# The third sort of a graph network kernel runs on into the first attention

## The chip, the cores and the metric

The kernel runs on one core of one Trainium2 chip. The metric is the device time of one launch in microseconds (us), the median of three runs. Engines are named as in the profile: PE is TensorE, DVE is VectorE, ACT is ScalarE, POOL is GpSimd, SP is SyncE.

## The reference

A graph has N = 3125 nodes with 64 features and E = 100000 directed edges (`src`, `dst`). Four layers run one after another, each on the normalised features and each added to them; the first is the one that matters here:

```
# layer 0: attention over all edges, both directions (200000 rows), 4 heads of 16
ngl, ngr = node_attr @ Wl.T, node_attr @ Wr.T
score = (att * leaky_relu(ngl[src] + ngr[dst], 0.2)).sum(-1)
alpha = softmax of score over the edges of one source node
out   = segment_sum(ngr[dst] * alpha, src)      # then an MLP with gelu, added to x
# layers 1, 2: three sums over neighbours (nbr_x of h, twice, and of the features)
nbr_x = segment_sum(h[src], dst) * inv_deg ;  nbr_r = segment_sum(edge_attr, dst) * inv_deg
# layer 3: attention again, over one direction, 8 heads of 64; its MLP and norms
```

## The kernel before

**The first attention.** Both directions of the edges are sorted by node and laid out in rows of 4 edges. 54 blocks (`NB0`) are worked off in order; a block is 8 rows of 4 edges in each of 128 partitions. For a block POOL issues 32 indirect DMAs (`gather`, L738), which fetch 128 rows of the node table each into one of four buffers `G0[:, r]`; SP loads the block's indices `jst` and own rows (`load_block`, L563, L564), ahead by three blocks; DVE computes scores, running maxima and weighted sums (`block0`, `scores`); ACT does the exponentials; SP stores the block. POOL may start block g when DVE has finished block g-4 (semaphore `av`), and when the `jst` of block g has landed. SP loads `jst` of block g once DVE has formed the own rows of block g-3 (semaphore `aow`, L1387).

**The third sort.** Before that, DVE sorts three arrays of 128 x 1024 keys with a bitonic network: two of them for the attention's rows, the third for layers 1 and 2. A sort is a list of 175 stages: compares within a partition (`compare`, L1203, L1206, L1212, each a few min and max instructions between two buffers), sign flips (L1220), and turns (`turn_over`, L1231, L1233), in which PE transposes the array through PSUM (L1855) and DVE copies it back. All of it stands in DVE's stream before block 0. The buffers of all three sorts are `SBL`, in the space of `oh`, and PE transposes into `acc`.

**The count matrices.** When the third sort has ended, SP stores the sorted keys (L584); POOL, after the gathers of blocks 0 to 2 and before those of block 3, fetches nine windows of them (`gather_keys`, L728); PE transposes these, and DVE takes them apart into the table `SD` (L1344 to L1355). From `SD` the attention's blocks make, beside their own work, 272 units: a comparison on DVE (`matrix_ones`, L1414), 8 products on PE (L1902), a copy and a store to `mt_dram` on ACT. Blocks also sum the edge attributes: 122 groups of records (`rec_ones`, L1423; on PE L1910). A block of the first 48 takes 5 units and 2 records; the last six take 6, 5, 5, 6, 5, 5 units and 4, 5, 4, 5, 4, 4 records. Blocks 4 to 47 are loops of four blocks on every engine; the first four and the last six are written out.

**The order inside a block on DVE** is: own rows (8 x L1387), then, once the 32 gathers have landed, L1437 to L1444 and the small ones up to L1408, then units (L1414), records (L1423), and, with ACT's exponentials, L1453, L1460 and the scan L1467. Nearly every DVE instruction waits for the one before it.

Of the kernel before, what the change touches and what calls it, by code (L numbers as in the profile page):

```python
# [22 lines left out]
P = 128  # L23
NC = -(-N // P)
# [3 lines left out]
EP = P  # L28
EC = 784
EF = E // EP  # L30
EX = E - EF * EP
GT = 8
# [47 lines left out]
UAT = (0, 5, 10, 15, 20)  # L80
UL = (0, 6, 11, 16, 22, 27, 32)
ULR = (0, 4, 9, 13, 18, 22, 26)
LAST = NB0 - 6
assert LAST % 4 == 0 and NU == UAT[4] * (LAST // 4) + UL[-1] and UAT[4] % 4 == 0 and 2 * LAST + ULR[-1] == NG
# [4 lines left out]
def build(nc, t, out):  # L89
# [3 lines left out]
    with ctx:  # L93
# [124 lines left out]
        KI = ohf_[:, 0:MT].bitcast(I)  # L218
        KI2 = OHXf[:, 6400:6400 + MT // 2].bitcast(I)
# [11 lines left out]
        TK = OHXf[:, 2048:2048 + NKB * TE]  # L231
# [157 lines left out]
        def spans(eng, n, ahead, step):  # L389
# [6 lines left out]
            with eng.Fori(1, whole) as i:  # L396
                for t in range(4):
                    at(i, t)
            for t in range(4 * whole, n):
                at(t // 4, t % 4)  # L400
# [13 lines left out]
        class Unit:  # L414

            def __init__(self, i, at):
                self.u, self.q, self.slot, self.turn = i * UAT[4] + at, at % 2, at % 4, i * (UAT[4] // 4) + at // 4

        def units_of(a):
            if isinstance(a.g, int) and a.g >= LAST:  # L420
                return [Unit(LAST // 4, k) for k in range(UL[a.g - LAST], UL[a.g - LAST + 1])]
            return [Unit(a.i, k) for k in range(UAT[a.t], UAT[a.t + 1])]

        class Recs:

            def __init__(self, i, at):
                self.g, self.r, self.q, self.turn = i * 8 + at, at % 4, at % 2, i * 2 + at // 4

# [42 lines left out]
        def _(sp):  # L471
# [111 lines left out]
            sp.wait_ge(S["sorted"], 3)  # L583
            sp.dma_start(keyd.rearrange("(p x) -> p x", p=P), SBL[l_at]).then_inc(S["lnd"], 16)  # L584
# [16 lines left out]
            spans(sp, NB0, 3, serve0)  # L601
# [58 lines left out]
        def _(gp):  # L660
# [126 lines left out]
        def _(act):  # L787
# [64 lines left out]
            def weights0(a):  # L852
# [17 lines left out]
                store_unit(ready)  # L870
# [45 lines left out]
        def _(v):  # L916
# [305 lines left out]
            def turn_over(bufs, m=None):  # L1222
# [3 lines left out]
                for q in range(dst.shape[-1] // 512):  # L1226
                    banks[0] += 1
                    v.wait_ge(S["stp"], banks[0])
                    o, i = dst[:, q * 512:(q + 1) * 512], acc[:, q * 512:(q + 1) * 512]
# [9 lines left out]
            def ordered(bufs, lg):  # L1239

                at[0] = 0
                for k in range(1, lg + 8):
                    m = k - lg
                    if m == 0:
                        signed(bufs, m)
                    if m > 0:
                        turn_over(bufs)
                        for q in reversed(range(m)):
                            compare(bufs, 1 << q, 1 << m if m < 7 else None)
                        turn_over(bufs, m if m < 7 else None)  # L1250
                    for q in reversed(range(min(k, lg))):
                        compare(bufs, 1 << q, 1 << k if k < lg else None)
                    if 0 <= m < 7:
                        signed(bufs, m)

            for l in range(2):
# [10 lines left out]
                ordered(SBL, LL)  # L1267
# [60 lines left out]
            v.wait_ge(S["lnd"], 2 * 16)  # L1328
            link(V.memset(SBL[0], float(NC << 19)))
            keys = SBL[0][0:EP, 0:EC]  # L1330
# [3 lines left out]
            empty(SBL[0], float(NC << 19))  # L1334
            V.memset(vdum[:, 1:2], 0.0).then_inc(S["cb"], 1)
            v.wait_ge(S["cb"], 1)
            ordered(SBL, LL)
# [4 lines left out]
            for k in range(2):  # L1342
                o = TK[:, k * 1024:(k + 1) * 1024].rearrange("p (k x) -> p k x", x=TE)
                link(V.tensor_tensor(o, o, cell14[:, k * 4:k * 4 + 4].unsqueeze(2).to_broadcast([P, 4, TE]), ALU.subtract))  # L1344
            o = TK[0:LASTP, (NKB - 1) * TE:NKB * TE]
            V.tensor_scalar(o, o, cell14[0:LASTP, NKB - 1:NKB], None, ALU.subtract).then_inc(S["sub"], 1)
            v.wait_ge(S["sub"], 2)
            whole = KI[:, 0:2 * P * (NKB - 1)].rearrange("p (k s e) -> p k e s", s=P, e=2)
            link(V.tensor_copy(whole, acc[:, :].rearrange("p (k e s) -> p k e s", e=2, s=P)))
            link(V.tensor_copy(KI[:, 2 * P * (NKB - 1):MT].rearrange("p (s e) -> p e s", e=2), pt[:, 0:2 * LASTP].rearrange("p (e s) -> p e s", e=2)))  # L1350
            of_unit = SD.rearrange("p (u o t e) -> p u o t e", o=2, t=GT, e=2)
            for o, val, op in ((0, 127, ALU.bitwise_and), (1, 7, ALU.logical_shift_right)):
                for h in range(2):
                    link(V.tensor_scalar(KI2, KI[:, h * (MT // 2):(h + 1) * (MT // 2)], val, None, op))
                    link(V.tensor_copy(of_unit[:, h * (NU // 2):(h + 1) * (NU // 2), o],  # L1355
                                       KI2.rearrange("p (u t) -> p u t", t=GT).unsqueeze(3).to_broadcast([P, NU // 2, GT, 2])))
            link(V.tensor_copy(iota_ps, iota1))
            link(V.tensor_copy(attb_ps, attb[:]))

# [67 lines left out]
            def block0(a):  # L1427
# [324 lines left out]
        def _(pe):  # L1752
# [99 lines left out]
            def turn_blocks(src, count, first=0):  # L1852

                for b in range(count):
                    last = nc.tensor.transpose(acc[:, (first + b) * P:(first + b + 1) * P], src[:, b * P:(b + 1) * P], ident[:])  # L1855
                    if b % 4 == 3:
                        last.then_inc(S["stp"], 1)

            def sort_turns(bufs, lg):

                at = lg * (lg + 1) // 2
                for m in range(1, 8):
                    turns[0] += 1
                    pe.wait_ge(S["srt"], turns[0])
                    turn_blocks(bufs[at % 2], 1 << (lg - 7))
                    at += 1 + m
                    turns[0] += 1
                    pe.wait_ge(S["srt"], turns[0])
                    turn_blocks(bufs[at % 2], 1 << (lg - 7))
                    at += 1 + lg  # L1870
                turns[0] += 1
                pe.wait_ge(S["srt"], turns[0])
                return at % 2

            for l in range(2):
                k = sort_turns(SBL, LL)
                assert k == l_at
# [4 lines left out]
            k = sort_turns(SBL, LL)  # L1882
            assert k == l_at
            pe.wait_ge(S["sub"], 1)
            for b in range(2 * (NKB - 1)):
                nc.tensor.transpose(acc[:, b * P:(b + 1) * P], TK[:, b * P:(b + 1) * P], ident[:])
            for e in range(2):
                last = nc.tensor.transpose(pt[:, e * LASTP:(e + 1) * LASTP], TK[0:LASTP, (NKB - 1) * TE + e * P:(NKB - 1) * TE + (e + 1) * P],
                                           ident[0:LASTP, 0:LASTP])
            last.then_inc(S["sub"], 1)  # L1890

            pe.wait_ge(S["moh"], 1)
            for k in range(4):
                nc.tensor.matmul(acc[:, k * 512:(k + 1) * 512], zrow[0:1, 0:P], zrow[0:1, :], start=True, stop=True, skip_group_check=True)

            def beside0(a):

                for c in units_of(a):
# [143 lines left out]
```

## Time and profile before

| | |
|---|---|
| median of 3 runs | 6147.66 us (6140.43 to 6149.96) |
| the profiled execution | 6139.35 us, of which the span is 6137.6 |
| busy: DVE, POOL, PE, ACT | 4092.7, 3783.2, 2661.9, 1253.9 us |
| gathers of the first attention | 1323.4 to 3713.8 us in the span |
| indirect gathers of both attentions (L738) | 2592, 1036 ns each in the mean |

All times inside the kernel are microseconds from the start of the span of one profiled execution. "Idle before" an instruction is the time in which its engine did nothing, with what ended it behind the arrow. "issue" stands for time in which nothing was waited for: for POOL the 0.30 us between two indirect DMAs.

### The profile page before, as it was taken

How to read it: one execution, taken by the hardware profiler on the slowest of the kernel's cores; microseconds unless marked ns; L12 is line 12 of the kernel's file. 1: busy time of each engine (PE TensorE's matmuls, PEld its weight loads, DVE VectorE, ACT ScalarE, POOL GpSimd, SP SyncE). 2: the span in 40 equal slices, each digit the busy share in tenths (PEclk: the TensorE clock that was granted, in tenths of full speed). 3: DMA queues.
4: the chain of work that ended last, by engine and by line, in shares of the span. 5: the costliest groups of instructions: out<-in, count | busy, mean ns of one | idle time of the engine just before them, and what ended most of it. 6: DMA issues, size and time to landing. Idle time of an engine off the chain costs nothing.

```text
span 6137.6 us, 56339 instructions
## 1 busy us (share of the span) xinstructions
PE 2661.9 (43%) x13332; PEld 1809.3 (29%) x13333; DVE 4092.7 (67%) x6865; ACT 1253.9 (20%) x4370; POOL 3783.2 (62%) x3760
## 2 busy tenths in 40 slices
PE   1785101011332322222222342677674577777746
PEld 0661101011322222222222242546453232332315
DVE  9778888886986776767676774232322576676655
ACT  0000000000111111111111110000000677777741
POOL 2777777776777777777777774000002777777730
PEclk6555555555555555555555555767685788888876
DMA  6221121211222222222222231435261222332230
GB/s 229 53 54 51 48 56 48 73 29 50 77 79 61 72 61 71 63 70 64 69 64 68 66 85 39 144 104 179 69 205 22 58 83 77 87 86 77 84 98 7
DMA packets 388365, 472.44 MB, mean 77 GB/s; under 512 B 212478, under 2 KB 248384, under 8 KB 381041
## 3 DMA queue, kind: packets, MB, share of 16 engines
q1 hardware_dynamic: 132624, 279.73, 13.8%
q0 software_dynamic: 114832, 129.82, 9.7%
q10 hardware_dynamic: 140752, 61.28, 3.5%
q14 instruction: 116, 0.94, 0.0%
q8 instruction: 41, 0.67, 0.0%
HBM read 291.34 MB, written 179.19 MB: 77 GB/s over the span
## 4 chain that ended last, share of the span: by engine, by line
POOL 58%; issue 21%; PE 9%; DMA 6%; DVE 5%; ACT 0%; POOLq 0%; DVEq 0%; ACTq 0%; SPq 0%
POOL arena L738 44%; POOL rec_dram L695 11%; PE acc L1959 4%; DMA oh<-mt_dram 2%; PE acc L1780 2%; DMA V<-in_edge_attr_dram 2%; DMA rec_dram<-V,rowst 1%; PE acc L1782 1%; PE acc L1943 1%; POOL own_dram L715 1%; POOL pdum L688 1%; POOL arena L765 1%; DVE arena L1579 1%; PE pt L1770 0%; POOL own_dram L769 0%
## 5 line engine op out<-in xcount | busy, mean ns | idle before, releaser
L738 POOL DMA_INDIRECT arena<-tab_dram,jst x2592 | 2685.8, 1036 | 778.3 <-issue 777.8
L695 POOL DMA_INDIRECT rec_dram<-V,rowst x784 | 866.1, 1105 | 229.9 <-issue 217.8
L688 POOL TENSOR_TENSOR pdum<-pdum 128x1 f32<-128x1 f32 x197 | 58.5, 297 | 1138.3 <-DVE arena L1607 864.6
L1902 PE MATMUL pw<-OHX 128*128 128x128 bf16 x1632 | 210.3, 310 | 1120.8 <-DVE OHX L1414 1120.8
L1902 PEld LDWEIGHTS pw<-OHX 128*128 128x128 bf16 x1632 | 156.9, 140 | 1172.3 <-DVE OHX L1414 859.7
L1910 PE MATMUL acc<-arena,oh 128*128 128x64 f32 x1952 | 427.1, 420 | 20.9 <-DVE oh L1423 20.7
L1910 PEld LDWEIGHTS acc<-arena,oh 128*128 128x128 f32 x1952 | 417.2, 330 | 34.9 <-issue 34.9
L900 ACT ACTIVATE arena<-arena,ew 128x64 f32<-128x64 f32 x1728 | 417.8, 333 | 33.3 <-PE acc L1983 33.3
L1437 DVE TENSOR_TENSOR arena<-arena,pt 128x1024 f32<-128x1024 f32 x108 | 131.8, 1221 | 431.7 <-DMA arena<-tab_dram,jst 429.4
L900 ACT ACTIVATE OHX<-arena,ew 128x64 f32<-128x64 f32 x1728 | 417.7, 333 | 2.5
L1983 PE MATMUL acc<-OHX,ident 128*128 128x512 f32 x432 | 253.7, 753 | 371.0 <-ACT OHX L900 371.0
L1855 PE MATMUL acc<-ident,oh 128*128 128x128 f32 x336 | 82.7, 427 | 752.3 <-DVE vdum L1224 752.3
L1212 DVE TENSOR_TENSOR oh<-oh 128x256 f32<-128x256 f32 x792 | 341.6, 431 | 37.8
L1855 PEld LDWEIGHTS acc<-ident,oh 128*128 128x128 f32 x336 | 65.9, 223 | 770.2 <-DVE vdum L1224 770.2
L855 ACT ACTIVATE arena<-dc 128x476 f32<-128x476 f32 x54 | 57.5, 1065 | 1143.3 <-DVE dc L1405 1143.3
L1959 PE MATMUL acc<-V,oh 128*128 x1440 | 234.7, 321 | 106.4 <-DVE arena L1579 86.5
L1579 DVE TENSOR_TENSOR arena<-arena,acc 128x192 f32 x360 | 127.6, 355 | 214.2 <-PE acc L1959 207.7
L1414 DVE TENSOR_TENSOR OHX<-iotab,OHX 128x2048 bf16<-128x2048 bf16 x204 | 249.7, 1224 | 28.0 <-DVE OHX L1414 15.6
L1983 PEld LDWEIGHTS acc<-OHX,ident 128*128 128x128 f32 x432 | 103.8, 248 | 520.1 <-issue 520.1
L825 ACT COPY V<-arena 128x8 f32 (+1 forms) x98 | 20.1, 205 | 1157.6 <-DMA rec_dram<-V,rowst 1080.5
L1902 PE MATMUL pw<-oh 128*128 128x128 bf16 x544 | 70.2, 310 | 386.2 <-DVE oh L1414 386.2
L1049 DVE TENSOR_TENSOR OHX<-iotab,arena 128x364 bf16<-128x364 bf16 x336 | 180.3, 536 | 64.5 <-DVE OHX L1049 17.9
(523 smaller groups left out, 6463.2 us busy)
## 6 DMA issues: line engine op xcount, KB each, us to landing
oh<-mt_dram SPq DMA_DIRECT2D x90, 512.0 KB, 3.6
arena<-tab_dram,jst POOLq DMA_INDIRECT x2592, 2.5
arena<-rec_dram SPq DMA_DIRECT2D x122, 288.0 KB, 3.6
mt_dram<-oh ACTq DMA_DIRECT2D x272, 128.0 KB, 1.7
oh<-mt_dram SPq DMA_DIRECT2D x75, 416.0 KB, 3.9
oh<-mt_dram SPq DMA_DIRECT2D x75, 384.0 KB, 4.0
rows_dram<-V SPq DMA_DIRECT2D x27, 1056.0 KB, 4.0
rows_dram<-arena SPq DMA_DIRECT2D x27, 1056.0 KB, 4.3
```

What stands on the lines that cost most here:

```text
L695: gp.indirect_dma_start(rec[:, :], bass.IndirectOffsetOnAxis(ap=rowst[:, q, k:k + 1], axis=0), recst[:, q, k, :], None).then_inc(S[f"scat{ ...
L738: gp.indirect_dma_start(hd.G[:, a.r, j, :], None, table[:, :], row_of(jst[:, a.r, j:j + 1])).then_inc(S[f"{x}g{a.r}"], 16)
L900: last = A.activation(V3r[vslot[f]][:, (k * H3 + h) * D:(k * H3 + h + 1) * D], G3[:, a.r, t, 0:D], ACT.Copy, scale=ew[:, a.q, t * H3 + h:t ...
L1049: V.tensor_tensor(paired(o[:, a:a + n]), iota_pairs(n, wide, EP), values[:, k, :].unsqueeze(2).to_broadcast([EP, n, wide // 2, 2]), ALU.is ...
L1212: V.tensor_tensor(o[r], a[r], b[r], op).then_inc(S["v"], 1)
L1414: V.tensor_tensor(paired(mones[c.slot].rearrange("p o t n -> p (o t) n")), iota_pairs(2 * GT, P), SD[:, bass.ds(c.u * (4 * GT), 4 * GT)].r ...
L1579: V.tensor_tensor(o, o, group_sum(g), ALU.add).then_inc(S["cadd"], 1)
L1855: last = nc.tensor.transpose(acc[:, (first + b) * P:(first + b + 1) * P], src[:, b * P:(b + 1) * P], ident[:])
L1902: last = nc.tensor.matmul(unit_bank(c.slot)[:, k // 2 * P:(k // 2 + 1) * P], mones[c.slot][:, 0, k, :], mones[c.slot][:, 1, k, :], start=k ...
L1910: last = nc.tensor.matmul(o, roh[:, c.q, k, :], RG[:, c.r, k, 0:D], start=False, stop=True, skip_group_check=True)
L1959: last = nc.tensor.matmul(group_sum(g), mring[:, slot, g * 4 + k, :], hsp[:, bass.ds(rows[g * 4 + k] * (3 * D), 3 * D)], start=k == 0, sto ...
L1983: last = nc.tensor.matmul(row_bank(2 * f + k // RK), ident[:], V3r[vslot[f]][:, k * 512:(k + 1) * 512], start=k % RK == 0, stop=k % RK == ...
```

## The change

The stages of the sort become a list. The third sort uses two buffers of its own, `SB3`, in the space of `OHX`, and PE transposes it into `pw`. Its first 104 stages (`SORT_FRONT`) stay ahead of block 0; the other 71 are spread over blocks 0 to 7 (`SORTED_IN`), 8 or 9 in each, between scores and records. SP stores the keys between its steps for blocks 7 and 8; POOL gathers the windows after block 11 (`KEYS_AT` = 12); they are turned and taken apart in three parts on DVE and PE in block 13 (`units_ready`, `units_turned`). Blocks 0 to 13 make no units; the 272 units are made in blocks 14 to 53, 6 or 7 in each, 7 in the last four. Records stay where they were. DVE, PE and ACT have all 54 blocks written out, without loops; POOL and SP keep theirs, split in two.

```diff
-UAT = (0, 5, 10, 15, 20)
-UL = (0, 6, 11, 16, 22, 27, 32)
+SORTED_IN, SORT_FRONT = 8, 104
+UNITS_AT, KEYS_AT = SORTED_IN + 6, SORTED_IN + 4
...
-        KI = ohf_[:, 0:MT].bitcast(I)
-        KI2 = OHXf[:, 6400:6400 + MT // 2].bitcast(I)
+        SB3 = [OHXf[:, k * SWL:(k + 1) * SWL] for k in range(2)]
+        KI, KI2 = [OHXf[:, k * 1024:(k + 1) * 1024].bitcast(I) for k in range(2)]
...
-        TK = OHXf[:, 2048:2048 + NKB * TE]
+        TK = OHXf[:, 4096:4096 + NKB * TE]
...
+        def unit_at(g):
+
+            return max(g - UNITS_AT, 0) * NU // (NB0 - UNITS_AT)
...
+        def sort_part(g):
+
+            rest = len(edge_sort) - SORT_FRONT
+            at_ = [0 if h < 0 else SORT_FRONT + rest * min(h, SORTED_IN) // SORTED_IN for h in (g, g + 1)]
+            return edge_sort[at_[0]:at_[1]]
...
         def first_attention(eng, body):
 
-            quads(eng, NB0, body, 0, LAST // 4)
-            for t in range(LAST, NB0):
+            for t in range(NB0):
                 body(Group(t // 4, t % 4))
...
-            sp.wait_ge(S["sorted"], 3)
-            sp.dma_start(keyd.rearrange("(p x) -> p x", p=P), SBL[l_at]).then_inc(S["lnd"], 16)
...
-            spans(sp, NB0, 3, serve0)
+
+            def store_keys():
+
+                sp.wait_ge(S["sorted"], 3)
+                sp.dma_start(keyd.rearrange("(p x) -> p x", p=P), SB3[l_at]).then_inc(S["lnd"], 16)
+            spans(sp, NB0, 3, serve0, SORTED_IN, store_keys)
...
-                quads(gp, n, rows)
+                if hd is heads0:
+                    quads(gp, n, rows, 0, KEYS_AT // 4)
+                    held[0] += KEYS_AT
+                    gather_keys()
+                    held[0] -= KEYS_AT
+                    quads(gp, n, rows, KEYS_AT // 4)
+                else:
+                    quads(gp, n, rows)
...
             def taken0(a):
 
-                if isinstance(a.g, int) and a.g == 3:
-                    held[0] += 3
-                    gather_keys()
-                    held[0] -= 3
                 after(gp, S["av"], a.g - 3)
...
-            ordered(SBL, LL)
-            assert at[0] == l_at
-            V.memset(vdum[:, 0:1], 0.0).then_inc(S["srt"], 1)
-            V.memset(vdum[:, 1:2], 0.0).then_inc(S["sorted"], 1)
-            v.wait_ge(S["tkg"], NKB * 16)
+            at[0] = 0
+            ordered(SB3, edge_sort[0:SORT_FRONT])
...
+            def sort_more(a):
+
+                at[0] = edge_at[0]
+                ordered(SB3, sort_part(a.g))
+                edge_at[0] = at[0]
+                if a.g == SORTED_IN - 1:
+                    assert at[0] == l_at
+                    V.memset(vdum[:, 1:2], 0.0).then_inc(S["sorted"], 1)
+
+            def units_ready():
+
+                v.wait_ge(S["tkg"], NKB * 16)
...
+                for part in range(3):
+                    v.wait_ge(S["sub"], 2 * part + 2)
...
+                    V.tensor_copy(ordered_, turned_).then_inc(S["sub"], 1)
+                    v.wait_ge(S["sub"], 2 * part + 3)
+                    for o, val, op in ((0, 127, ALU.bitwise_and), (1, 7, ALU.logical_shift_right)):
+                        link(V.tensor_scalar(KI2[:, 0:wide], KI[:, 0:wide], val, None, op))
+                        link(V.tensor_copy(of_unit[:, part * P:part * P + wide // GT, o],
+                                           KI2[:, 0:wide].rearrange("p (u t) -> p u t", t=GT).unsqueeze(3).to_broadcast([P, wide // GT, GT, 2])))
...
                 scores(heads0, a, st, summed)
+                if a.g < SORTED_IN:
+                    sort_more(a)
+                if a.g == UNITS_AT - 1:
+                    units_ready()
                 for c in units_of(a):
                     matrix_ones(c)
...
+            side[0] = 0
+            sort_turns(pw, SB3, edge_sort[0:SORT_FRONT])
...
             def beside0(a):
 
+                if a.g < SORTED_IN:
+                    sort_turns(pw, SB3, sort_part(a.g))
+                if a.g == UNITS_AT - 1:
+                    units_turned()
```

## Rows read from the trace of the kernel before

**Rows 1.** The page's part 4, the chain that ended last, by engine.

```profile
POOL 58%; issue 21%; PE 9%; DMA 6%; DVE 5%; ACT 0%; POOLq 0%; DVEq 0%; ACTq 0%; SPq 0%
```

**Rows 2.** POOL's waits, 1324 to 3715: total us, times, longest us.

```profile
POOL pdum L688 <- DMA jst<-meta_dram: 28.9, 1, 28.9
```

**Rows 3.** Timeline of POOL, 1323 to 3715: start, us, engine, line, operation.

```profile
1323.39 0.48 POOL L688 TENSOR_TENSOR pdum<-pdum 128x1 f32<-128x1 f32 x1 [5.37 <-DMA jst<-meta_dram]
...
1456.87 0.74 POOL L688 TENSOR_TENSOR pdum<-pdum 128x1 f32<-128x1 f32 x3
...
1467.88 0.91 POOL L728 DMA_INDIRECT OHX<-keys_dram,arena  x1 [0.30 <-issue]
1497.68 0.19 POOL L688 TENSOR_TENSOR pdum<-pdum 128x1 f32<-128x1 f32 x1 [28.89 <-DMA jst<-meta_dram]
...
3712.89 0.94 POOL L738 DMA_INDIRECT arena<-tab_dram,jst  x1 [0.30 <-issue]
```

**Rows 4.** Timeline of SP's queue, 1290 to 1560.

```profile
1436.95 0.33 SPq L584 DMA_DIRECT2D keys_dram<-oh  x1
...
1494.07 0.33 SPq L563 DMA_DIRECT2D jst<-meta_dram  x1
```

**Rows 5.** Timeline of DVE, 1311 to 1560.

```profile
1315.63 0.69 DVE L1231 COPY oh<-acc 128x512 f32<-128x512 f32 x1 [1.21 <-PE acc L1855]
...
1317.21 7.53 DVE L1212 TENSOR_TENSOR oh<-oh 128x256 f32<-128x256 f32 x16
...
1342.30 0.75 DVE L1220 TENSOR_SCALAR oh<-oh,sgn 128x1024 f32<-128x1024 f32 x1
...
1436.84 0.06 DVE L1340 MEMSET vdum<- 1x1 f32 x1
1470.42 2.49 DVE L1344 TENSOR_TENSOR OHX<-OHX,arena 128x1024 f32<-128x1024 f32 x2 [33.51 <-DMA OHX<-keys_dram,arena]
...
1491.46 2.59 DVE L1387 SCALAR_TENSOR_TENSOR pt<-pt,jst,arena 128x64 f32<-128x64 f32 x8
...
1528.03 2.59 DVE L1387 SCALAR_TENSOR_TENSOR pt<-pt,jst,arena 128x64 f32<-128x64 f32 x8
...
1558.80 1.29 DVE L1467 TENSOR_TENSOR_SCAN V<-arena 128x544 f32<-128x544 f32 x1
```

**Rows 6.** DVE's waits, 1324 to 3757.

```profile
DVE arena L1437 <- DMA arena<-tab_dram,jst: 429.4, 43, 11.0
```

**Rows 7.** The page's part 5: busy us, mean ns | idle before.

```profile
L1414 DVE TENSOR_TENSOR OHX<-iotab,OHX 128x2048 bf16<-128x2048 bf16 x204 | 249.7, 1224 | 28.0 <-DVE OHX L1414 15.6
```

**Rows 8.** Groups of POOL's instructions, 1396 to 1406, DVE comparing.

```profile
L738 POOL DMA_INDIRECT arena<-tab_dram,jst x8 | 9.2, 1155 | 2.4 <-issue 2.4
```

**Rows 9.** Groups of POOL's instructions, 1437 to 1457, DVE idle.

```profile
L738 POOL DMA_INDIRECT arena<-tab_dram,jst x16 | 15.1, 944 | 4.9 <-issue 4.9
```

**Rows 10.** Timeline of POOL, one gather beside DVE's L1220.

```profile
1342.65 1.22 POOL L738 DMA_INDIRECT arena<-tab_dram,jst  x1 [0.30 <-issue]
```

**Rows 11.** Groups of DVE's instructions, 1454 to 1498.

```profile
L1355 DVE CAST OHX<-OHX 128x2176 bf16<-128x2176 int32 x4 | 5.2, 1294 | 0.1
L1354 DVE TENSOR_SCALAR OHX<-oh 128x1088 int32<-128x1088 int32 x4 | 2.9, 727 | 0.1
```

**Rows 12.** Timeline of DVE, the last blocks (51, 52, 53).

```profile
3628.36 2.59 DVE L1387 SCALAR_TENSOR_TENSOR pt<-pt,jst,arena 128x64 f32<-128x64 f32 x8
...
3672.48 2.59 DVE L1387 SCALAR_TENSOR_TENSOR pt<-pt,jst,arena 128x64 f32<-128x64 f32 x8
...
3702.22 1.22 DVE L1423 TENSOR_TENSOR oh<-pt,arena 128x1024 f32<-128x1024 f32 x1 [2.19 <-PE acc L1910]
...
3711.86 2.59 DVE L1387 SCALAR_TENSOR_TENSOR pt<-pt,jst,arena 128x64 f32<-128x64 f32 x8
3716.24 2.47 DVE L1437 TENSOR_TENSOR arena<-arena,pt 128x1024 f32<-128x1024 f32 x2 [1.79 <-DMA arena<-tab_dram,jst]
...
3751.61 1.29 DVE L1467 TENSOR_TENSOR_SCAN V<-arena 128x544 f32<-128x544 f32 x1
```

More of the change, by code:

```diff
@@ L387, in quads, with spans @@
                     body(Group(n // 4, t))
-        def spans(eng, n, ahead, step):
+        def spans(eng, n, ahead, step, cut=4, between=None):
             def at(i, t):
@@ L395, in spans @@
                 at(0, t)
-            with eng.Fori(1, whole) as i:
-                for t in range(4):
-                    at(i, t)
+            for i, e in ((1, cut // 4), (cut // 4, whole)):
+                if i == cut // 4 and between:
+                    between()
+                if i + 1 == e:
+                    for t in range(4):
+                        at(i, t)
+                elif i < e:
+                    with eng.Fori(i, e) as turn:
+                        for t in range(4):
+                            at(turn, t)
             for t in range(4 * whole, n):
@@ L414, in build, with __init__ @@
         class Unit:
[L416 to L417 removed]
+            def __init__(self, at):
+                self.u, self.q, self.slot, self.turn = at, at % 2, at % 4, at // 4
         def units_of(a):
[L420 to L422 removed]
+            return [Unit(k) for k in range(unit_at(a.g), unit_at(a.g + 1))]
         class Recs:
@@ L427, in __init__, with sort_stages @@
                 self.g, self.r, self.q, self.turn = i * 8 + at, at % 4, at % 2, i * 2 + at // 4
+        def unit_at(g):
+            return max(g - UNITS_AT, 0) * NU // (NB0 - UNITS_AT)
+        def sort_stages(lg):
+            for k in range(1, lg + 8):
+                m = k - lg
+                if m == 0:
+                    yield "sign", 0, None
+                if m > 0:
+                    yield "turn", None, None
+                    for q in reversed(range(m)):
+                        yield "compare", 1 << q, 1 << m if m < 7 else None
+                    yield "turn", m if m < 7 else None, None
+                for q in reversed(range(min(k, lg))):
+                    yield "compare", 1 << q, 1 << k if k < lg else None
+                if 0 < m < 7:
+                    yield "sign", m, None
+                if m == 0:
+                    yield "sign", 0, None
+        edge_sort = list(sort_stages(LL))
+        def sort_part(g):
+            rest = len(edge_sort) - SORT_FRONT
+            at_ = [0 if h < 0 else SORT_FRONT + rest * min(h, SORTED_IN) // SORTED_IN for h in (g, g + 1)]
+            return edge_sort[at_[0]:at_[1]]
         def recs_of(a):
@@ L1237, in turn_over, with ordered @@
                 at[0] = 1 - at[0]
[L1239 to L1254, printed above, removed]
+            def ordered(bufs, stages):
+                for what, b, c in stages:
+                    if what == "turn":
+                        turn_over(bufs, b)
+                    elif what == "sign":
+                        signed(bufs, b)
+                    else:
+                        compare(bufs, b, c)
             for l in range(2):
@@ L1342, in _ @@
[L1342 to L1356, printed above, removed]
+            at[0] = 0
@@ L1850, in _, with turn_blocks, sort_turns @@
             turns = [0]
-            def turn_blocks(src, count, first=0):
+            def turn_blocks(into, src, count):
                 for b in range(count):
-                    last = nc.tensor.transpose(acc[:, (first + b) * P:(first + b + 1) * P], src[:, b * P:(b + 1) * P], ident[:])
+                    last = nc.tensor.transpose(into[:, b * P:(b + 1) * P], src[:, b * P:(b + 1) * P], ident[:])
                     if b % 4 == 3:
                         last.then_inc(S["stp"], 1)
[L1859 to L1870, printed above, removed]
+            side = [0]
+            def sort_turns(into, bufs, stages):
+                for what, _, _ in stages:
+                    if what == "turn":
+                        turns[0] += 1
+                        pe.wait_ge(S["srt"], turns[0])
+                        turn_blocks(into, bufs[side[0]], SWL // P)
+                    if what != "sign":
+                        side[0] = 1 - side[0]
+            for l in range(2):
+                side[0] = 0
+                sort_turns(acc, SBL, sort_stages(LL))
+                assert side[0] == l_at
                 turns[0] += 1
                 pe.wait_ge(S["srt"], turns[0])
[L1873 to L1877, printed above, removed]
             pe.wait_ge(S["mlb"], 1)
@@ L1881, in _, with units_turned @@
             last.then_inc(S["mlm"], 1)
[L1882 to L1892, printed above, removed]
+            side[0] = 0
+            sort_turns(pw, SB3, edge_sort[0:SORT_FRONT])
             for k in range(4):
                 nc.tensor.matmul(acc[:, k * 512:(k + 1) * 512], zrow[0:1, 0:P], zrow[0:1, :], start=True, stop=True, skip_group_check=True)
+            def units_turned():
+                pe.wait_ge(S["sub"], 1)
+                for part in range(3):
+                    if part:
+                        pe.wait_ge(S["sub"], 2 * part + 1)
+                    n = P if part < 2 else LASTP
+                    for b in range(8 if part < 2 else 2):
+                        at_ = (part * 8 + b) * P
+                        last = nc.tensor.transpose(pw[:, b * n:(b + 1) * n], TK[0:n, at_:at_ + P], ident[0:n, 0:n])
+                    last.then_inc(S["sub"], 1)
             def beside0(a):
+                if a.g < SORTED_IN:
+                    sort_turns(pw, SB3, sort_part(a.g))
+                if a.g == UNITS_AT - 1:
+                    units_turned()
                 for c in units_of(a):
```

29 lines of the change are left out of this document (21 added, 8 removed).

## The prediction

> **What bounds the kernel now.** I read the chain of waits first: 58% of the span is POOL, and most of the 21% "issue" is the pause between its indirect DMAs [rows 1]. Then POOL's waits over the first attention: from its first gather to its last it waits for another engine once, 28.9 us, before block 3 [rows 2]. Everything else there is POOL at its own pace. The timeline of POOL shows where that wait stands: gathers of blocks 0 to 2 from 1323.4 to 1456.9, nine windows of keys up to 1468.8, nothing until 1497.7, and from there 51 blocks without a pause up to 3713.8 [rows 3]. So (3713.8 - 1497.7) / 51 = 43.45 us a block.
>
> What the wait is for needs SP's and DVE's timelines. SP loads the `jst` of block 3 at 1494.07 [rows 4], when DVE has formed the own rows of block 0, which start at 1491.46 [rows 5]. DVE is that late because it ends the third sort at 1436.9, waits 33.5 us for the windows of keys, and then prepares the units [rows 5]. Once the blocks run, DVE is the one that waits: 429.4 us in 43 waits for the gathers [rows 6]. A block with 5 units and 2 records takes it 1560.1 - 1528.0 = 32.1 us [rows 5]. What this change can win is therefore the 28.9 us of POOL, and nothing that only shortens DVE.
>
> **Part 1: the wait before block 3.** After the change DVE leaves the sort after stage 104. By the list this is the first compare behind the turn whose copies start at 1315.6; a compare is four instructions of the sixteen at 1317.2, so 1.9 us, and the front ends at 1319.1 [rows 5]. Some 3 us of small copies and memsets follow. The first gather starts at 1323.4 as before [rows 3]: it waits for SP's loads, not for the sort. Own rows of block 0 are made at about 1327, SP loads block 3's `jst` right then, and POOL comes to block 3 only at 1323.4 + 3 x 43.45 = 1454. The wait is gone: **-28.9**. The nine windows are fetched later and cost POOL the same 12 us (1456.9 to 1468.8) in either place [rows 3]. Their keys are stored by SP behind block 7, near 1715; POOL asks for them after block 11, near 1845. DVE wants them in block 13, near 1945. None of the three waits. SP's new wait for the sorted keys stands behind its store of block 7, which itself waits for DVE's end of block 7, so nothing is queued behind it for long.
>
> **Part 2: is DVE quick enough in blocks 0 to 7?** A unit is 1224 ns and a gap of 0.03, 1.25 us [rows 7]; a block without its 5 units takes 32.1 - 6.3 = 25.8 us. The rest of the sort took 1436.9 - 1319.1 = 117.8 us, turns with their waits for PE included [rows 5]; that is 14.7 us in each of eight blocks. Sum 40.5 us, against POOL's 43.45: DVE still waits for gathers, by some 3 us a block. And there is a cushion. Block 0's gathers land near 1366 (1323.4, 40.4 for 32 gathers beside an idle DVE as in part 3, and the 2.4 us from the last gather's end to L1437 [rows 3, 12]) and DVE is through with it 40.5 - 2.6 us later, near 1404; POOL needs that only when it comes to block 4, near 1497, 93 us later. A turn waits 1.21 us for PE [rows 5]; the records of the block before, which PE works off in order, have long been done by then. In block 13 DVE has the preparation to do: about 20 us (it took 1470.4 to 1491.5 before [rows 5], and now goes to PE and back twice more), 46 us in all, within the cushion. In blocks 14 to 52 it has 6.8 units: 25.8 + 8.5 = 34.3 us. POOL never waits: cost nothing, hidden under 43.45 us of gathers. Without that cover (a block over 43.45 + 93 / 8 = 55 us) every further us counts eight times.
>
> **Part 3: DVE's work slows POOL's issue.** A gather takes 944 ns while DVE is idle [rows 9], 1155 ns while it compares [rows 8]: with the 0.30 us pause, 0.21 us in 1.45, or 0.145 for each us of compares. Over whole blocks it is less: 32 gathers at 1.24 us and the 0.6 us instruction ahead make 40.4 us, so 32.1 us of mixed DVE work cost 3.05, 0.095 for each us. One gather beside a 0.75 us L1220, which reads and writes SBUF at about 1.4 elements a ns, took 1.22 us [rows 5, 10]: 0.28 for 0.75, or 0.37 for each us. The total of DVE's work is unchanged, so only what before lay in POOL's pause, or ahead of its first gather, counts:
>
> - L1354 and L1355, 8.1 us [rows 11], the nearest row is L1220's: 8.1 x 0.37 = 3.0
> - L1344 and the copies out of PSUM, about 5.4 us, at 0.1 to 0.145: 0.7
> - the sort between 1319.1 and 1323.4, and own rows and L1437 of block 0 between 1491.5 and 1497.7: 4.3 x 0.145 + 6.2 x 0.095 = 1.2
>
> Together **+4.9**. From below the bound is nothing, if PSUM and cast operands don't disturb; from above 10, if L1354 and L1355 stop POOL altogether. I take 4.9 since a row of the same kind gives it.
>
> The Trainium skill (SBUF — State Buffer, "Who interferes with whom") says that a DVE instruction in a 2-port mode holds the port pair that GpSimd needs for its descriptors, and that GpSimd then fully blocks. It also says that `tensor_tensor` did not delay descriptors in its probe; the trace differs, 1155 ns against 944 beside compares. By the page's rule the 8.1 us would cost 8.1, not 3.0.
>
> **Part 4: the end of the attention.** The last four blocks have 7 units instead of 6, 5, 5 in blocks 51, 52, 53. DVE is nearly as slow as POOL there: 44.1 us for block 51 and 39.4 for block 52, since each record past the second waits for PE, 2.19 + 1.22 us [rows 12]. Into block 53 it had 1.79 us to spare. It gets 1 + 2 units more before that, 3.75 us, so it begins 2.0 us late, and has 2 more units, 2.5 us, behind the last gather. **+4.5**. Bounds: 2.5 (if it isn't late) and 6 (if blocks 48 to 50 with 4 more units leave it behind already; they should take 41.9, 44.1 and 41.9, together less than 3 x 43.45).
>
> **Loops written out.** No loop is left on DVE, PE and ACT, so more code streams in. The last six blocks were written out before and show no gap over 0.03 us between dependent instructions [rows 12]; cost nothing, hidden anyway under POOL. Behind the attention nothing is touched.
>
> **Sum.** -28.9 + 4.9 + 4.5 = -19.5 us. The profiled execution took 6139.35, so it would become 6119.9; it is the fastest of those shown, 8.3 below their median of 6147.66. From the median: **6128 us**.
>
> **The rivals.**
>
> - *Forecast*, gain 13 to 25 us: 0.70.
> - *Full stop*: each DVE instruction of the kind of L1354 and L1355 stops POOL for its whole length, in the case of the 8.1 us that move under gathers. Against it: 1.22 us beside L1220, which would have had to be 1.69. Gain 28.9 - 8.1 - 1.9 - 4.5 = 14.4, time 6133: 0.08. It is what the Trainium skill's page on SBUF, named above, would give.
> - *Larger gain*: the moved work disturbs no gather and DVE isn't late at the end: 28.9 - 2.5 = 26, time 6121: 0.10.
> - *The wait stays or moves*: POOL is held before block 3 or 4 for as long by another step of the chain DVE, SP, `jst` (SP loads blocks in order, and its step for block 0 stands behind the waits for `cb` and the records' scatters). Then only the costs are left, +9.4, time 6157. The trace speaks against it, where SP's load at 1494.07 stands right behind the own rows' end, 1491.46 + 2.59 [rows 4, 5]: 0.06.
> - *Slower*: DVE becomes the bound in blocks 0 to 7. It decides from 55 us a block on. At 60 us POOL waits 8 x 16.5 - 93 = 39 us in blocks 4 to 8, the sum is -28.9 + 39 + 9.4 = +19.5, time 6167. It would take a PE that answers each turn behind 7 us of records (four times 1.75 us each, two turns in a block at most: 14 us, 54.5 in all), and more beside it. The order inside the block speaks against it: 0.03.
> - *Written-out code stalls* DVE by over 9 us a block, from block 14 on: 0.03, slower too by what is over.
>
> **Numbers.** The three runs lie within 10 us of each other, so 0.2%, 12.3 us, is about what can be told from no change. The forecast's bounds are 28.9 - 1 - 2.5 = 25 and 28.9 - 10 - 6 = 13, times 6122 to 6135; with 5 us for the spread of the runs on either side the range is 6117 to 6139. Faster by over 0.2%: 0.70 + 0.10 and half of the full stop, less what the spread takes, 0.82. Same: 0.14. Slower: 0.04.
>
> **What the profile after would show.** No wait of POOL before block 3 and none for DVE, last gather at 3713.8 - 28.9 + 4.9 = 3690; DVE's wait for gathers in each of blocks 1 to 7, a few us; keys fetched near 1845; blocks 8 to 13 gathered in about 42 us each, those from 14 on in 44; from the last gather to the last L1467 43.6 instead of 39.1 us [rows 3, 12]. The prediction is wrong if POOL shows a wait for DVE in blocks 4 to 11, if the gathers of blocks 0 to 7 take over 45 us, or if DVE runs late by more than a few us into block 53.

## The result, and the profile after

The changed kernel takes 6082.2 us (6076.4 to 6084.2, 4 runs) against 6148.0 before on the same chip: the ratio is 0.9894, 95% interval 0.9877 to 0.9911, 66 us faster. The forecast was 6128, 20 us faster; the time lies far below its range. Measured again later the ratio was 0.9892 (0.9876 to 0.9909).

The page of the profile after, its part 4 (answers to [rows 1]) and, from part 5, the gathers of both attentions (busy us, mean ns | idle before):

```profile
POOL 52%; issue 20%; DVE 10%; PE 10%; DMA 6%; ACT 0%; POOLq 0%; DVEq 0%; ACTq 0%; SPq 0%
...
L775 POOL DMA_INDIRECT arena<-tab_dram,jst x2592 | 2643.3, 1020 | 778.2 <-issue 778.0
```

Before, these 2592 gathers, 1036 ns each, were busy for 2685.8 us. They have become 42 us shorter, without one fewer. The forecast had them 4.9 us longer.

POOL's waits after, 1324 to 3640 (answers to [rows 2]):

```profile
POOL arena L775 <- issue: 518.2, 1726, 0.4
POOL OHX L765 <- issue: 2.7, 9, 0.3
```

The 28.9 us before block 3 are gone, and no other wait has come. POOL's timeline after (answers to [rows 3]): the first gather, the last window of keys and the instruction ahead of block 12, the last gather.

```profile
1322.98 0.19 POOL L725 TENSOR_TENSOR pdum<-pdum 128x1 f32<-128x1 f32 x1 [5.44 <-DMA jst<-meta_dram]
...
1852.25 0.91 POOL L765 DMA_INDIRECT OHX<-keys_dram,arena  x1 [0.30 <-issue]
1853.18 0.20 POOL L725 TENSOR_TENSOR pdum<-pdum 128x1 f32<-128x1 f32 x1
...
3640.37 0.94 POOL L775 DMA_INDIRECT arena<-tab_dram,jst  x1 [0.30 <-issue]
```

From the first instruction to the end of the last gather it is 3641.3 - 1323.0 = 2318.3 us, where it was 3713.8 - 1323.4 = 2390.4 [rows 3]: 72 less, of which the wait is 28.9. From block 14 on a block's gathers take 42.6 us, where the forecast had 44. SP's queue after (answers to [rows 4]): block 3's `jst` and the keys.

```profile
1326.75 0.33 SPq L597 DMA_DIRECT2D jst<-meta_dram  x1
...
1710.93 0.45 SPq L637 DMA_DIRECT2D keys_dram<-OHX  x1
```

DVE's timeline after (answers to [rows 5, 12]): the end of what stands ahead of block 0, the own rows of block 0 and the wait for its gathers, the wait in block 1, and the last block.

```profile
1321.58 0.06 DVE L1419 MEMSET vdum<- 1x1 f32 x1
1324.14 2.58 DVE L1438 SCALAR_TENSOR_TENSOR pt<-pt,jst,arena 128x64 f32<-128x64 f32 x8 [2.50 <-DMA arena<-own_dram]
1364.93 2.48 DVE L1488 TENSOR_TENSOR arena<-arena,pt 128x1024 f32<-128x1024 f32 x2 [38.20 <-DMA arena<-tab_dram,jst]
...
1409.91 2.47 DVE L1488 TENSOR_TENSOR arena<-arena,pt 128x1024 f32<-128x1024 f32 x2 [4.59 <-DMA arena<-tab_dram,jst]
...
3645.04 2.58 DVE L1438 SCALAR_TENSOR_TENSOR pt<-pt,jst,arena 128x64 f32<-128x64 f32 x8
3647.65 2.47 DVE L1488 TENSOR_TENSOR arena<-arena,pt 128x1024 f32<-128x1024 f32 x2
...
3685.54 1.29 DVE L1522 TENSOR_TENSOR_SCAN V<-arena 128x544 f32<-128x544 f32 x1
```

In block 0 and in five of blocks 1 to 7 DVE waits for gathers (4.59 us in block 1), so it keeps up. At the end it is late: L1488 of block 53 starts 6.3 us after the last gather, where its counterpart started 2.4 us after. From the last gather to the end of the last scan it is 3686.8 - 3641.3 = 45.5 us, before 39.1 [rows 3, 12].

### The profile page after: what moved, and what is told of

Read it like the earlier page. It is cut to its first block, busy times and chain, and to the rows that moved or that the text cites. A ratio compares the mean times of both kernels' runs of the same rounds, so it can differ in the third digit from the quotient of the medians.

```text
span 6074.7 us, 53421 instructions
## 1 busy us (share of the span) xinstructions
PE 2659.3 (44%) x13332; PEld 1808.0 (30%) x13333; DVE 4093.2 (67%) x6869; ACT 1254.0 (21%) x4370; POOL 3739.8 (62%) x3760
## 4 chain that ended last, share of the span: by engine, by line
POOL 52%; issue 20%; DVE 10%; PE 10%; DMA 6%; ACT 0%; POOLq 0%; DVEq 0%; ACTq 0%; SPq 0%
POOL arena L775 38%; POOL rec_dram L732 11%; PE acc L2020 3%; DMA oh<-mt_dram 2%; DMA V<-in_edge_attr_dram 2%; PE acc L1835 2%; DMA rec_dram<-V,rowst 2%; DVE OHX L1465 1%; PE acc L1837 1%; PE acc L2004 1%; POOL own_dram L752 1%; DVE arena L1634 1%; PE acc L1971 1%; POOL arena L805 1%; POOL pdum L725 1%
## 5 line engine op out<-in xcount | busy, mean ns | idle before, releaser
L775 POOL DMA_INDIRECT arena<-tab_dram,jst x2592 | 2643.3, 1020 | 778.2 <-issue 778.0
L1488 DVE TENSOR_TENSOR arena<-arena,pt 128x1024 f32<-128x1024 f32 x108 | 131.8, 1221 | 444.3 <-DMA arena<-tab_dram,jst 442.2
L1910 PE MATMUL acc<-ident,oh 128*128 128x128 f32 x224 | 55.1, 427 | 487.1 <-DVE vdum L1265 487.1
L1465 DVE TENSOR_TENSOR OHX<-iotab,OHX 128x2048 bf16<-128x2048 bf16 x204 | 249.6, 1224 | 5.9
L1253 DVE TENSOR_TENSOR oh<-oh 128x256 f32<-128x256 f32 x528 | 227.7, 431 | 24.6
L2004 PE MATMUL acc<-V,oh 128*128 128x192 bf16 x1875 | 174.7, 251 | 90.5 <-DMA oh<-mt_dram 53.1
L1515 DVE TENSOR_REDUCE arena<-V 128x544 f32<-128x2176 f32 x54 | 209.9, 3888 | 1.9
```

The source lines that it names most:

```text
L1253: V.tensor_tensor(o[r], a[r], b[r], op).then_inc(S["v"], 1)
L1465: V.tensor_tensor(paired(mones[c.slot].rearrange("p o t n -> p (o t) n")), iota_pairs(2 * GT, P), SD[:, bass.ds(c.u * (4 * GT), 4 * GT)].r ...
L1515: V.tensor_reduce(RS0.rearrange("p (x f) -> p f x", f=RB), V0.rearrange("p (f k) h e -> p f (h e) k", k=RK), AX, ALU.add).then_inc(S["ars" ...
L2004: last = nc.tensor.matmul(group_sum(a.t // 2), mring[:, a.t % 4, k, :], hsp[:, j * (3 * D):(j + 1) * (3 * D)], start=j == 0, stop=j == NC ...
```

## Why did the gathers become shorter?

Two timelines from the middle of the attention, a block with 5 units before and one with 7 after. Before, POOL and then DVE:

```profile
2600.75 1.93 POOL L738 DMA_INDIRECT arena<-tab_dram,jst  x1 [0.30 <-issue]
2602.98 1.08 POOL L738 DMA_INDIRECT arena<-tab_dram,jst  x1 [0.30 <-issue]
2604.36 1.07 POOL L738 DMA_INDIRECT arena<-tab_dram,jst  x1 [0.30 <-issue]
```

```profile
2602.01 1.22 DVE L1414 TENSOR_TENSOR OHX<-iotab,OHX 128x2048 bf16<-128x2048 bf16 x1 [0.16 <-DVE oh L1414]
2603.39 1.23 DVE L1414 TENSOR_TENSOR OHX<-iotab,OHX 128x2048 bf16<-128x2048 bf16 x1 [0.15 <-DVE OHX L1414]
2604.77 1.23 DVE L1414 TENSOR_TENSOR OHX<-iotab,OHX 128x2048 bf16<-128x2048 bf16 x1 [0.15 <-DVE OHX L1414]
```

After, POOL and then DVE (x3 stands for three in a row, 0.03 us apart):

```profile
2592.49 1.92 POOL L775 DMA_INDIRECT arena<-tab_dram,jst  x1 [0.30 <-issue]
2594.71 0.96 POOL L775 DMA_INDIRECT arena<-tab_dram,jst  x1 [0.30 <-issue]
2595.97 0.96 POOL L775 DMA_INDIRECT arena<-tab_dram,jst  x1 [0.30 <-issue]
```

```profile
2592.37 1.22 DVE L1465 TENSOR_TENSOR oh<-iotab,OHX 128x2048 bf16<-128x2048 bf16 x1
2593.62 3.75 DVE L1465 TENSOR_TENSOR OHX<-iotab,OHX 128x2048 bf16<-128x2048 bf16 x3
```

In both, gathers and comparisons run in step. Before, comparisons start 1.38 us apart and so do gathers; after, 1.25 and 1.26. A gather ends 0.83 us after a comparison ends (2603.23 to 2604.06 before, 2594.84 to 2595.67 after). POOL's own pace is 1.24 us, so a comparison every 1.25 us costs it nearly nothing, and one every 1.38 us costs 0.14. The looped blocks of before have the 0.15 us between comparisons, the ones written out 0.03. That is a reading; the experiments test it.

The whole traces bear it out. Of the 1728 gathers of the first attention, 267 before and 265 after have a comparison running 0.11 us after their start, and every one of them ends 0.81 to 0.84 us after that comparison does. The 367 and 354 that find DVE idle at that point take 0.94 to 0.97 us. Not every DVE instruction does this: the 161 and 160 gathers that meet the long reduction (L1460, after it L1515) take 0.94 to 0.96 us too.

What the change took away are small lengthenings: gathers of 0.96 to 1.3 us held 49 us beyond 0.944 each before and hold 17 after. The larger part it left: gathers of over 1.5 us, 143 of them before, held 133 us beyond 0.944, and every trace here has 132 to 145 of them.

## The experiments

Ratios are to the kernel before on the same chip, with the 95% interval.

**Writing out alone.** In the kernel before, all 54 blocks are written out, on DVE, PE and ACT (first run), on DVE alone (second), on PE and ACT alone (third). Nothing else is changed.

```diff
         def first_attention(eng, body):
 
+            if eng is nc.vector:        # third run: is not
+                for t in range(NB0):
+                    body(Group(t // 4, t % 4))
+                return
             quads(eng, NB0, body, 0, LAST // 4)
```

> The kernel before with one edit: all 54 blocks of the first attention are written out on DVE, PE and ACT, no loop left there. Sort, keys and units stay as before. Theory A (the gathers became quicker because the blocks' code is written out: beside a unit of the looped blocks a gather took 1.07 us, in the written-out ones 0.96): blocks 4 to 47 go from 43.2 to about 42.2 us each, 44 blocks, the time falls by 35 to 45 us to about 6108; POOL's 28.9 us wait before block 3 stays. Theory B (they became quicker because of where the units and the sort stand, or because of the other buffers): no change, 6140 to 6150.

> The kernel before with the 54 blocks written out on DVE alone; PE and ACT keep their loops. Theory A1 (it is DVE's own spacing: between two unit comparisons 0.15 to 0.25 us in the loop, 0.03 us written out): the same gain as with all three written out, 35 to 45 us. Theory A2 (PE or ACT in loops answer later and so space DVE out): no gain. Theory B: no gain.

> The kernel before with the 54 blocks written out on PE and ACT alone; DVE keeps its loop. Theory A1: no change, within 3 us of the kernel before. Theory A2: the whole gain of 35 to 45 us. Theory B: no change.

Measured: all three engines 6106.1 us, 0.9931 (0.9915 to 0.9948); DVE alone 6107.5, 0.9938 (0.9921 to 0.9955); PE and ACT alone 6146.7, 0.9998 (0.9988 to 1.0008). So some 40 of the 66 us come from DVE's code being written out, with sort, keys and units where they were. The gathers between 1940 and 3580 us show it; the rows are of before, DVE alone, PE and ACT alone, and the changed kernel (busy us, mean ns | idle before):

```profile
L738 POOL DMA_INDIRECT arena<-tab_dram,jst x1209 | 1270.7, 1051 | 362.9 <-issue 362.9
```

```profile
L742 POOL DMA_INDIRECT arena<-tab_dram,jst x1231 | 1263.4, 1026 | 369.4 <-issue 369.4
```

```profile
L742 POOL DMA_INDIRECT arena<-tab_dram,jst x1210 | 1269.7, 1049 | 363.1 <-issue 362.9
```

```profile
L775 POOL DMA_INDIRECT arena<-tab_dram,jst x1231 | 1261.6, 1025 | 369.3 <-issue 369.2
```

25 ns less in the mean for each of 32 x 44 gathers of the looped blocks is 35 us. It isn't spread evenly: in blocks 16 to 47 the 160 gathers that overlap a comparison are 107 ns shorter with DVE written out, the other 864 only 10, so two thirds of the gain stand beside the comparisons. The wait before block 3 stayed in the written-out kernel, as it should; its waits of POOL:

```profile
POOL pdum L687 <- DMA jst<-meta_dram: 28.4, 1, 28.4
```

**The spacing by itself.** In the changed kernel two small dependent memsets behind each comparison, then one:

```diff
                 v.wait_ge(S["moh"], c.u + 1)
+                for k in range(2):          # later run: one
+                    link(V.memset(vdum[:, 3:4], 0.0))
```

> The changed kernel with two tiny dependent memsets (1 x 1, some 0.09 us each) behind each of the 272 unit comparisons on DVE, so that these come 1.42 instead of 1.25 us apart, about as in the loops of before (1.38 to 1.47). It computes the same. DVE has room for it: 34 + 1.2 us of a block's 42. Theory A1 (POOL's gathers fall in step with DVE's comparisons, so that a wider spacing lengthens each gather beside them): gathers beside units go from 0.96 to about 1.1 us, 272 x 0.15 = some 40 us slower than the changed kernel, 6120. Theory A2 or B (spacing of DVE has no part in it): at most 3 us slower, by the 14 x 0.09 us behind the last gather.

> The changed kernel with one tiny dependent memset behind each unit comparison, where an earlier run had two: the comparisons come some 1.34 us apart instead of 1.25 or 1.49. If a gather beside them takes on their spacing (1.25 is POOL's own pace), it becomes 1.34 - 0.30 = 1.04 us, 272 x 0.09 = 24 us in all and a few at the end: about a third of the 67 us that two memsets cost, a ratio of 0.993 to 0.994 to the kernel before. If it is any second instruction between them that costs, not the time: nearly all of the 67 us.

Measured: two memsets 6149.6 us, 1.0002 (0.9992 to 1.0011), 67 us above the changed kernel; one memset 6110.8, 0.9942 (0.9926 to 0.9959), 30 us above it. Both lost more than expected, since the comparisons came further apart than planned. With two, POOL and DVE:

```profile
2618.99 1.18 POOL L775 DMA_INDIRECT arena<-tab_dram,jst  x1 [0.30 <-issue]
2620.47 1.19 POOL L775 DMA_INDIRECT arena<-tab_dram,jst  x1 [0.30 <-issue]
```

```profile
2618.12 1.23 DVE L1465 TENSOR_TENSOR OHX<-iotab,OHX 128x2048 bf16<-128x2048 bf16 x1
2619.40 0.17 DVE L1470 MEMSET vdum<- 1x1 f32 x2
2619.61 1.23 DVE L1465 TENSOR_TENSOR OHX<-iotab,OHX 128x2048 bf16<-128x2048 bf16 x1
```

With one:

```profile
2607.93 1.06 POOL L775 DMA_INDIRECT arena<-tab_dram,jst  x1 [0.30 <-issue]
2609.30 1.07 POOL L775 DMA_INDIRECT arena<-tab_dram,jst  x1 [0.30 <-issue]
```

```profile
2606.95 1.23 DVE L1465 TENSOR_TENSOR OHX<-iotab,OHX 128x2048 bf16<-128x2048 bf16 x1
2608.23 0.06 DVE L1469 MEMSET vdum<- 1x1 f32 x1
2608.33 1.23 DVE L1465 TENSOR_TENSOR OHX<-iotab,OHX 128x2048 bf16<-128x2048 bf16 x1
```

Comparisons are 1.49 and 1.38 us apart here (with one memset 1.37 in the median of all), gathers 1.48 and 1.37. DVE had time for the memsets in either case (POOL had no wait for it): what they cost they cost POOL, 272 x (1.49 - 1.25) = 65 us and 272 x (1.37 - 1.25) = 33 us, close to the 67 and 30 measured. The kernel with one memset is written out and yet has the gather lengths of a loop, so it is the spacing that counts and not the loop.

**The change with DVE's loop kept.** Blocks 16 to 47 of the changed kernel go back into a loop of four on DVE, with 7 units in each (14 units in the two blocks ahead, 34 in the last six; the unit's number is computed from the turn, which the diff leaves out).

```diff
+            if eng is nc.vector:
+                for t in range(16):
+                    body(Group(t // 4, t % 4))
+                quads(eng, NB0, body, 4, LAST // 4)
+                for t in range(LAST, NB0):
+                    body(Group(t // 4, t % 4))
+                return
```

> The changed kernel with blocks 16 to 47 put back into a loop of four on DVE alone, 7 units in each of them (in all 272 as before: 14 in blocks 14 and 15, 224 in the loop, 34 in the last six). Sort, keys and unit preparation as in the changed kernel. Theory A1 (DVE's spacing in a loop lengthens the gathers beside it): 32 blocks at 43.3 instead of 42.3 us, some 30 us slower than the changed kernel, 6112; with the 12 more blocks that before had in its loop this is what was predicted for the change. If it is not DVE's loop: 6082 within 3.

Measured 6108.6 us, 0.9947 (0.993 to 0.9963), 0.0053 above the changed kernel's 0.9894, or 33 us. In its trace the stretch of gathers is 26 to 31 us longer than in the two traces of the changed kernel. On DVE the spaces are back, here in a looped block:

```profile
2609.79 1.23 DVE L1478 TENSOR_TENSOR oh<-iotab,OHX 128x2048 bf16<-128x2048 bf16 x1 [0.24 <-DVE OHX L1478]
```

**Is it the splitting of the sort that takes the wait away?** All 175 stages ahead of block 0, the rest as in the changed kernel.

```diff
-SORTED_IN, SORT_FRONT = 8, 104
+SORTED_IN, SORT_FRONT = 8, 175
```

> The changed kernel with all 175 stages of the third sort ahead of block 0 (in the new buffers); keys still fetched after block 11, units from block 14. Theory C (the 28.9 us wait of POOL came from the fetching and taking apart of the keys ahead of block 0, not from the sort): block 0 begins at about 1440, its own rows are made before POOL comes to block 3 at 1454, its end near 1466 lies before block 4's start at 1497, so POOL has no wait and the time is that of the changed kernel within 5 us, 6077 to 6087. Theory D (it is the splitting of the sort that takes the wait away): POOL waits again before block 3 or 4, 15 to 30 us, 6097 to 6112.

> The changed kernel itself, so that the next runs are compared with it on one chip. Its ratio to the kernel before should be that of the first measurement, 0.9894, within 0.001.

> The kernel with the whole third sort ahead of block 0 once more, beside the changed kernel. Its trace has shown no wait of POOL before any block and gathers that end 7 us later than in the changed kernel. If the splitting of the sort is worth nothing in time: the same ratio as the changed kernel, within 0.0007. If the 7 us stand for it: 0.001 higher than the changed kernel's.

Measured: first 6083.7 us, 0.9906 (0.9889 to 0.9922); then, on one chip, the changed kernel 6081.2, 0.9892 (0.9876 to 0.9909), and the sort ahead 6084.5, 0.9905 (0.9888 to 0.9921). The intervals overlap; twice 0.0012 or 0.0013 stands between the two, but in the traces of the pair the last gather ends at 3647.0 in the changed kernel and at 3638.7 with the sort ahead, the other way round from the first pair (3641.3 and 3648.6). The times leave 0 to 8 us open for the splitting. The traces narrow it: the gathers of block 13, up to where the two kernels differ, end at 1936.9 and 1938.7 in the changed kernel and at 1940.1 and 1940.2 with the sort ahead, 1 to 3 us later. What else stands between the traces arises in blocks that are the same in both. The splitting is not worth 28.9. SP, DVE and POOL's waits of the second run with the sort ahead:

```profile
1442.43 0.33 SPq L597 DMA_DIRECT2D jst<-meta_dram  x1
```

```profile
1439.82 2.59 DVE L1438 SCALAR_TENSOR_TENSOR pt<-pt,jst,arena 128x64 f32<-128x64 f32 x8
...
1464.50 1.29 DVE L1522 TENSOR_TENSOR_SCAN V<-arena 128x544 f32<-128x544 f32 x1
```

```profile
POOL arena L775 <- issue: 518.0, 1725, 0.4
POOL OHX L765 <- issue: 2.7, 9, 0.3
```

The sort ends at the same time as before; block 3's `jst` is loaded at 1442.4, 15 us before POOL is through with block 2 (1457.0), and block 0 is done at 1465.8, 34 us before POOL is through with block 3 (1500.0). The wait came from what stood between sort and block 0: fetching the windows behind the gathers of block 2, and taking them apart.

**The end of the attention.** Units: 8 in each of blocks 14 to 47, none in the last six; then also 4, 5, 5, 5, 5, 2 records there.

```diff
-            return max(g - UNITS_AT, 0) * NU // (NB0 - UNITS_AT)
+            return min(max(g - UNITS_AT, 0) * 8, NU)
...
-ULR = (0, 4, 9, 13, 18, 22, 26)
+ULR = (0, 4, 9, 14, 19, 24, 26)
```

> The changed kernel with 8 units in each of blocks 14 to 47 and none in the last six. If what stands behind the last gather is DVE's own work (45.5 us in the changed kernel, 7 units and a lateness of 3.9 us in it): 7 x 1.25 + 3.9 = 12.6 us less, 6069 to 6070. If 8 units a block slow the gathers more than 6.8 do, by something else than their number: nearer to 6082. If units stand elsewhere at no cost and the end hides them: 6082.

> The kernel of the run before with 4, 5, 5, 5, 5, 2 records in the last six blocks instead of 4, 5, 4, 5, 4, 4. Two records fewer behind the last gather, each 3.41 us (1.22 of DVE and 2.19 of waiting for PE): 6.8 us less than that run, 6063. The blocks with 5 records and no units take DVE 44.1 - 7.5 = 36.6 us, less than a block's gathers, so they should cost nothing; if they do, the gain is smaller.

> The changed kernel with 8 units in blocks 14 to 47, none in the last six, and 4, 5, 5, 5, 5, 2 records there, beside the changed kernel on one chip. From the last gather to the last scan its trace had 24.6 us against 45.5: 20 us less, a ratio 0.0033 below the changed kernel's.

Measured: units alone 6069.0 us, 0.9882 (0.9865 to 0.9898); with the records 6058.3, 0.9866 (0.985 to 0.9883), and again, beside the changed kernel, 6056.1, 0.9853 (0.9836 to 0.9869) against 0.9892. That is 25 us below the changed kernel and 87 below the kernel before: the fastest version here. Its last gather and last block, POOL and DVE:

```profile
3643.57 0.94 POOL L775 DMA_INDIRECT arena<-tab_dram,jst  x1 [0.30 <-DMA rows_dram<-arena]
```

```profile
3646.88 2.48 DVE L1488 TENSOR_TENSOR arena<-arena,pt 128x1024 f32<-128x1024 f32 x2 [4.24 <-DMA arena<-tab_dram,jst]
...
3668.65 1.29 DVE L1522 TENSOR_TENSOR_SCAN V<-arena 128x544 f32<-128x544 f32 x1
```

DVE waits for the last gathers again, 4.24 us, and is done 3669.9 - 3644.5 = 25.4 us after the last one instead of 45.5. The first comparison (6069.0) was of a chip on which the kernel before took 6140.2, so it is 7 us by ratio where 12.6 was expected, and its interval overlaps the changed kernel's: by the times alone this step isn't shown. In its trace 32.0 us lie behind the last gather (3644.8 to 3676.8), 13.5 less than in the changed kernel, while the gathers end 3.5 us later, which is within what they scatter by (3641.3 and 3647.0 in two traces of the changed kernel).

## Why the prediction was wrong

- *Part 1, the wait, -28.9: right.* POOL has no wait, the keys went at 1842 to 1853 (forecast 1845), SP stored them at 1711 (1715), and the windows cost POOL 12 us as before.
- *Part 2, DVE quick enough in blocks 0 to 7: right.* It waited for gathers in five of blocks 1 to 7, 2.9 to 5.2 us each; forecast were some 3 us in each. The three rivals that let POOL wait (the wait stays, slower, written-out code stalls) did not happen.
- *Part 3, gathers slowed by moved work, +4.9: too high as a sum.* In the written-out kernels the gathers took, from the start of the first to the end of the last, 2355.2 and 2349.8 us with the wait, that is 2326.8 and 2321.0 without it; in two traces of the changed kernel 2317.7 and 2322.7. The moved work costs between -9 and +2 us. The 5 us between the last two are six gathers: 133 of over 1.5 us in the first trace, 139 in the second.
- *The full stop, 8.1 us: ruled out.* In the changed kernel L1354 and L1355 have become L1407 and L1408 and stand under the gathers of block 13. POOL's group there (1955.4 to 1967), one of its gathers, and DVE beside it:

```profile
L775 POOL DMA_INDIRECT arena<-tab_dram,jst x7 | 9.5, 1358 | 2.1 <-issue 2.1
```

```profile
1959.88 1.65 POOL L775 DMA_INDIRECT arena<-tab_dram,jst  x1 [0.30 <-issue]
```

```profile
1959.49 1.23 DVE L1408 CAST OHX<-OHX 128x2048 bf16<-128x2048 int32 x1
```

Seven gathers of 0.944 us would be 6.6 us, so the two lines cost at most 2.9 us, not 8.1; the forecast had 3.0. The size was right, but not the form of the price, so much for each us of DVE: four of the seven gathers carry nearly all of it, and each of them ends 0.81 to 0.85 us after an L1408 does (1961.53 after 1960.72 here). A gather is held until one DVE instruction ends, not by each of them. The row that gave the price fits this too: L1220 ends at 1343.05 [rows 5] and the gather beside it at 1343.87 [rows 10].

- *Part 4, the end, +4.5: right mechanism, 6.4 measured.* DVE was 3.9 us late into block 53, not 2.0. Its blocks took what was forecast (42.1, 44.1 and 41.9 us for 48 to 50), but the sum set 43.45 us of gathers against them, the mean of blocks 3 to 53 of before; those of blocks 49 to 53 now took 42.2.
- *"Loops written out ... cost nothing, hidden anyway under POOL", and "nothing that only shortens DVE" can win: this step failed.* DVE's code has no cost of its own under POOL, but its spacing sets the length of POOL's gathers beside it, and writing out DVE alone won 39 us. I had the number in hand, 0.03 us between dependent instructions in the written-out blocks [rows 12], and took 1.25 us for a unit from [rows 7], which doesn't say so: it has 28.0 us idle ahead of 204 comparisons, 0.14 each, so 1.36 us for a unit in the mean of looped and written-out blocks. This was 40 us of the 66. The trace of before shows both kinds, in the groups of POOL's instructions between 1940 and 3455 us (looped) and between 3458 and 3714 (the last six blocks, written out):

```profile
L738 POOL DMA_INDIRECT arena<-tab_dram,jst x1115 | 1174.5, 1053 | 334.7 <-issue 334.7
```

```profile
L738 POOL DMA_INDIRECT arena<-tab_dram,jst x192 | 197.2, 1027 | 57.6 <-issue 57.6
```

For the same reason part 3's premise, "The total of DVE's work is unchanged, so only what before lay in POOL's pause, or ahead of its first gather, counts", was wrong: not the sum of DVE's work counts but how it lies against the gathers.

Without that step the sum holds as far as the noise lets one see. From the kernel before with all loops written out (0.9931) to the changed kernel (0.9892, 0.9894) there are 0.0037 to 0.0039, 23 to 24 us, where the sum said 19.5; each of these ratios is known to 0.0017, 10 us. And with 32 of the 44 looped blocks back in a loop the change gives 0.9947; an estimate of 1 us for each of the other twelve, from these 33 us for 32 blocks, makes it 0.9967, the forecast's ratio. That the parts meet so closely is partly luck: part 3 was too high and part 4 too low.

## What to carry to other kernels

When one engine sets the pace by many equal short instructions, look at what runs beside them in both the looped and the written-out part of the trace: the same instruction 25 ns longer in the mean, 1400 times, was worth more than the wait that the change was about. A wait before a block is charged to the work that stands directly ahead of it; move that first, and see whether the larger piece (here the sort) has to move at all. And what an engine does behind the last transfer is on the path even where the same work is free everywhere else.

## What the runs showed of the hardware

An indirect DMA's issue on POOL beside a run of DVE comparisons of two SBUF operands (128 x 2048, bf16) falls in step with them: it ends 0.81 to 0.84 us after a comparison ends, at 1.25, 1.37, 1.38 and 1.49 us of spacing alike, and the first one of a run, which begins 0.12 us after the first comparison does, takes 1.9 us. At these spacings a denser DVE thus made POOL faster. The Trainium skill (SBUF — State Buffer, "Who interferes with whom") says that `tensor_tensor` takes only the shared pair's read interface and did not stall descriptors; here the trace differs, 0.944 us beside an idle DVE [rows 9] against 1.07 and 1.19 beside spaced comparisons, and the measurement decides. That it is a lock taken in the gap between two DVE instructions would fit, but no run showed the lock itself. A gather also reads its indices (`jst`) from SBUF, and whether that read waits or the writing of the descriptors isn't shown either.

A long reduction on DVE (128 x 2176, f32, 3.9 us) lengthened none of the 161 gathers that began beside it (0.94 to 0.96 us).

In DVE's loops 0.15 to 0.24 us stood between dependent comparisons and 0.03 where the same code was written out. This was not at the loop's turn but between instructions inside it, and not between all: in the same looped blocks the eight dependent L1387 stand 0.035 us apart, though the values that they wait for are computed from the turn as well. So computed wait values alone don't explain it. The comparisons also have an operand whose address is computed, but 0.13 to 0.14 us stood ahead of L1453 and L1465 too, which have none. What in the loop's code takes the time was not tried apart.
